# Linear attention in chunks of 64 tokens instead of 128, in smaller TensorE tiles, in a fused attention and mixture-of-experts layer

## What is computed

```python
h = layernorm(x)
q, k = elu(h @ Wq.T) + 1, elu(h @ Wk.T) + 1; v = h @ Wv.T      # 16 heads of 16 features
for each token t, each head:                                   # causal linear attention
    KV += outer(k[t], v[t]);  Ks += k[t]
    o[t] = (q[t] @ KV) / (q[t] . Ks + 1e-8)
x = x + o @ Wo.T
h = layernorm(x)
cw = top-4 of 8 experts, out of the best 2 of 4 groups, by sigmoid(h @ gate_w.T) + bias; scaled to sum 2.5
x = x + sum_e cw[e] * mlp_e(h) + mlp_shared(h)                 # mlp: silu(h@Wg) * (h@Wu) @ Wd, 128 wide
```

## Time and profile before

| | |
|---|---|
| median of 3 runs | 1036.24 us (1032.89 to 1036.34) |
| the profiled execution, by the same clock as the runs | 1035.56 us |
| its span, first to last instruction | 1033.8 us |
| PE busy | 1007.7 us (97%), 8437 matmul records |
| DVE busy | 873.0 us (84%) |
| POOL, ACT busy | 537.8 us (52%), 422.6 us (41%) |
| granted TensorE clock | full (2.4 GHz) in all slices |

### The profile page before, as it was taken

How to read it: one execution, slowest core, us unless ns; L and a number is a source line. 1 busy time by engine, 2 the same in 40 slices (tenths; PEclk the granted TensorE clock), 3 DMA queues, 4 the chain that set the end, 5 groups by cost and what they waited for, 6 DMA issues and landing times.

```text
span 1033.8 us, 22214 instructions
## 1 busy us (share of the span) xinstructions
PE 1007.7 (97%) x8437; PEld 858.1 (83%) x8437; DVE 873.0 (84%) x1855; ACT 422.6 (41%) x750; POOL 537.8 (52%) x440
## 2 busy tenths in 40 slices
PE   6889999999999999999999999999999999999997
PEld 5667878888888888888888888888888888888886
DVE  5988998898888889989898988889889898887564
ACT  5755343443434344343444434244343434422222
POOL 5763545636455564445646454564445546443653
PEclk9999999999999999999999999999999999999999
DMA  5011424444242443324435252443424345241511
GB/s 204 2 47 43 106 60 133 83 103 111 60 138 63 132 105 96 100 63 134 83 103 113 58 138 63 142 94 99 100 64 136 76 103 113 58 118 36 130 60 64
DMA packets 235161, 96.49 MB, mean 93 GB/s; under 512 B 161712, under 2 KB 217520, under 8 KB 235056
## 3 DMA queue, kind: packets, MB, share of 16 engines
q1 hardware_dynamic: 235056, 95.07, 36.0%
HBM read 66.60 MB, written 28.44 MB: 92 GB/s over the span
## 4 chain that ended last, share of the span: by engine, by line
PE 87%; DVE 6%; DMA 2%; ACT 1%; issue 1%; POOL 1%; SPq 1%; DVEq 0%; ACTq 0%
PE bank L989 53%; PE y_bank L989 19%; PE bank L1098 6%; PE bank L1114 5%; PE bank L1085 2%; PE bank L1128 2%; PE bank L1140 1%; DMA cw_all<-cw_dram 1%; DMA cw_all<-in_w_qkvo 1%; DVE scores L860 1%; DMA x_dram<-blocks 0%; DMA expo<-x_dram 0%; DVE den L869 0%; POOL et L729 0%; DVE et L957 0%
## 5 line engine op out<-in xcount | busy, mean ns | idle before, releaser
L989 PE MATMUL bank<-xt_hi,wg_hi 128*128 128x512 f32 x576 | 237.1, 412 | 3.0 <-DVE et L957 2.3
L989 PE MATMUL bank<-xt_hi,wg_lo 128*128 128x512 f32 x576 | 228.1, 396 | 0.0
L989 PE MATMUL bank<-xt_lo,wg_hi 128*128 128x512 f32 x576 | 227.8, 396 | 0.0
L732 POOL TENSOR_TENSOR h_lo<-et,h_hi 128x512 fp32r<-128x512 f32 x142 | 181.1, 1293 | 89.6 <-ACT h_hi L682 89.4
L729 POOL TENSOR_TENSOR et<-et,cw_all 128x512 f32<-128x512 f32 x126 | 166.2, 1338 | 112.6 <-DVE et L963 94.4
L860 DVE TENSOR_TENSOR scores<-bank,cst 128x512 f32<-128x512 f32 x240 | 152.6, 681 | 35.6 <-PE bank L1098 29.4
L989 PE MATMUL y_bank<-wd_hi,h_hi 128*128 128x256 f32 x576 | 164.9, 286 | 0.0
L989 PE MATMUL y_bank<-wd_lo,h_hi 128*128 128x256 f32 x576 | 162.1, 281 | 0.0
L989 PE MATMUL y_bank<-wd_hi,h_lo 128*128 128x256 f32 x576 | 161.3, 280 | 0.0
L989 PEld LDWEIGHTS bank<-xt_hi,wg_hi 128*128 128x128 f32 x576 | 108.3, 188 | 41.3 <-issue 16.6
L682 ACT ACTIVATE h_hi<-et 128x512 fp32r<-128x512 f32 x144 | 86.1, 624 | 116.7 <-POOL et L729 55.9
(11 more groups left out here) (135 smaller groups left out, 1870.5 us busy)
## 6 DMA issues: line engine op xcount, KB each, us to landing
cw_all<-cw_dram SPq DMA_DIRECT2D x128, 256.0 KB, 3.9
x_dram<-blocks SPq DMA_DIRECT2D x112, 128.0 KB, 3.3
out_y<-x_mid SPq DMA_DIRECT2D x32, 256.0 KB, 4.8
x_in<-in_x SPq DMA_DIRECT2D x15, 512.0 KB, 5.3
num_t<-x_dram SPq DMA_DIRECT2D x15, 512.0 KB, 4.0
expo<-x_dram SPq DMA_DIRECT2D x13, 512.0 KB, 4.0
k_dram<-blocks SPq DMA_DIRECT2D x52, 96.0 KB, 2.6
k_tok<-k_dram SPq DMA_DIRECT2D x13, 384.0 KB, 3.4
```

Source lines behind the costliest of these rows:

```text
L732: nc.gpsimd.tensor_tensor(h_lo[:, i % HR, :], et[:, i % ET, :], h_hi[:, i % HR, :].bitcast(f32), ALU.subtract).then_inc(h_lo_done, 1)
L989: ins = nc.tensor.matmul(dst, l, r, start=first and n == 0, stop=last and n == 2, skip_group_check=shared)
```

## The change

The chunk becomes 64 tokens (`CH`), eight of them. `scores` uses tiles of 32 rows x 64 columns: the pair g picks the row group, and even and odd chunks (r = 0, 1) pick the column half, that is partitions 0 to 63 or 64 to 127 of the bank of g. `values` uses 64 rows x 32 columns: r picks the row half and g the column group, and even and odd chunks write to banks of their own (`o` 2i + r). `state` is one entry now, in tiles of 64 x 32 with 32 streamed columns and two banks. `inter` uses tiles of 32 x 32 on the diagonal: pair g in row group g and column group g, seven chunks, even and odd chunks in the two `o` banks. The masks are 64 wide, so that there are 8 of 128 x 512 per batch in place of 16. DVE adds the seven states up in seven instructions. `k_turn` and `blocks.2`/`put.2`/`get.2` move four subtiles of k in place of three. `mult` is four instructions of 128 x 256 in place of two of 128 x 512. The last batch's weight rows 4 to 7 go to ring buffers of `scores`, once `values` of that batch is done with them, and wait for no `weigh`.

All order tables and `BANK` are written anew. One line of each, before and after:

```diff
-        up.6.3 down.3.3 state.1.1 down.4.3 scores.2.1 values.0.1 values.1.1 down.5.3 inter.0.1 inter.1.1
+        down.3.3 up.8.3 down.4.3 scores.1.1 down.5.3 down.6.3 values.0.1 values.1.1 router.0.2 inter.1.1
...
-        turn.0.0 turn.1.0 warm.17.0 v.1.0 k.0.0 q.0.0 v.0.0 k.1.0 q.1.0 scores.0.0 k_turn.0.0 scores.1.0
+        turn.1.0 turn.0.0 warm.21.0 k.0.0 q.0.0 q.1.0 k.1.0 warm.20.0 k_turn.1.0 k_turn.0.0 scores.0.0 v.0.0
...
-    ("o", 1): 2, ("q", 0): 5, ("q", 1): 5, ("router", 0): 1, ("scores", 0): 0, ("scores", 1): 4, ("scores", 2): 3,
+    ("o", 1): 5, ("o", 2): 1, ("o", 3): 3, ("q", 0): 2, ("q", 1): 4, ("router", 0): 0, ("scores", 0): 3,
```

The code (a line "..." stands where lines are left out):

```diff
+CH = P // 2
+CHUNKS = S // CH
...
     if name == "scores":
         return [("scores", 4 * i + g) for g in range(4)]
     if name == "values":
-        return [("o", i // 2)] if i % 2 == 0 else []
+        return [("o", 2 * i), ("o", 2 * i + 1)]
+    if name == "state":
+        return [("state", 0), ("state", 1)]
     return [(name, i)] if name in BANKED else []
+
+def product_range(*sizes):
+    return itertools.product(*(range(n) for n in sizes))
...
+        def cw_extra(k):
+            return scores[:, k, :, :].rearrange("p a q -> p (a q)")
...
+            k = slot_weights(i, b) - 1
+            if b == B - 1 and k >= CW:
+                wait_for(eng, cw_last[k - CW], 16)
+                return cw_extra(k)
+            n = E * b + k
...
+        def ring(i, b):
+            return scores[:, (PAIRS * b + i) % SM, :, :]
+        def wait_scores(eng, i, b):
+            before, j = divmod(PAIRS * b + i - SM, PAIRS)
+            if before >= 0:
+                wait_filled(eng, "values", j // 4, before)
...
-                        wait_weighed(sp, e % E + int(e // E < B - 1), e // E)
-                    sp.dma_start(cw_all[:, i % CW, :], cw_dram[b % 2, i].partition_broadcast(P))\
-                        .then_inc(cw_loaded[i % CW], 16)
+                    if b == B - 1 and i >= CW:
+                        wait_filled(sp, "values", 0, b)
+                        wait_filled(sp, "values", 1, b)
+                        dst, landed_sem = cw_extra(i), cw_last[i - CW]
+                    else:
+                        if E * b + i >= CW:
+                            before, j = divmod(E * b + i - CW, E)
+                            wait_weighed(sp, j + 1, before)
+                        dst, landed_sem = cw_all[:, i % CW, :], cw_loaded[i % CW]
+                    sp.dma_start(dst, cw_dram[b % 2, i].partition_broadcast(P)).then_inc(landed_sem, 16)
...
-                    dve.wait_ge(filled, FILLED["state", i, b])
-                    wait_filled(dve, "inter", 2 * i, b - 1)
-                    wait_filled(dve, "inter", 2 * i + 1, b - 1)
-                    nc.vector.tensor_tensor(st[:, i, :, :],
-                                            bank[BANK["state", i]][:, 0:(SUBS - 1) * P]
-                                            .rearrange("p (c n) -> p c n", n=P),
-                                            block_mask.unsqueeze(1).broadcast_to([P, SUBS - 1, P]), ALU.mult)\
-                        .then_inc(drained[BANK["state", i]], 1)
-                    dve.wait_ge(drained[BANK["state", i]], USES["state", i, b])
-                    nc.vector.tensor_tensor(st[:, i, 1, :], st[:, i, 0, :], st[:, i, 1, :], ALU.add)\
-                        .then_inc(state_done, 1)
-                    dve.wait_ge(state_done, 2 * STATE["state", i, b] - 1)
-                    nc.vector.tensor_tensor(st[:, i, 2, :], st[:, i, 1, :], st[:, i, 2, :], ALU.add)\
-                        .then_inc(state_done, 1)
+                    dve.wait_ge(filled, FILLED["state", 0, b])
+                    wait_filled(dve, "inter", 0, b - 1)
+                    wait_filled(dve, "inter", 1, b - 1)
+                    even, odd = (bank[BANK["state", r]][:, 0:CH * SUBS].rearrange("p (c n) -> p c n", n=CH)
+                                 for r in range(2))
+                    nc.vector.tensor_copy(st_sum[:, 0, :], even[:, 0, :])
+                    nc.vector.tensor_copy(st_sum[:, 1:6:2, :], odd[:, 0:3, :]).then_inc(drained[BANK["state", 1]], 1)
+                    dve.wait_ge(drained[BANK["state", 1]], USES["state", 1, b])
+                    link(nc.vector.tensor_tensor(st_sum[:, 1:6:2, :], st_sum[:, 1:6:2, :], even[:, 0:3, :], ALU.add))
+                    link(nc.vector.tensor_tensor(st_sum[:, 3, :], st_sum[:, 1, :], st_sum[:, 3, :], ALU.add))
+                    link(nc.vector.tensor_tensor(st_sum[:, 5, :], st_sum[:, 3, :], st_sum[:, 5, :], ALU.add))
+                    nc.vector.tensor_tensor(st_sum[:, 2:7:2, :], st_sum[:, 1:6:2, :], even[:, 1:4, :], ALU.add)\
+                        .then_inc(drained[BANK["state", 0]], 1)
+                    dve.wait_ge(drained[BANK["state", 0]], USES["state", 0, b])
+                    nc.vector.tensor_tensor(st[:, :, :, :].rearrange("p c m n -> p (c m) n"),
+                                            st_sum.rearrange("p c (m n) -> p (c m) n", m=KC),
+                                            head_mask.unsqueeze(1).broadcast_to([P, (CHUNKS - 1) * KC, 2 * DH]),
+                                            ALU.mult).then_inc(state_done, 1)
+                    dve.wait_ge(state_done, STATE["state", 0, b])
...
-                    for j in (2 * i, 2 * i + 1):
-                        dve.wait_ge(filled, FILLED["values", j, b])
-                        dve.wait_ge(filled, FILLED["inter", j, b])
+                    dve.wait_ge(filled, FILLED["values", i, b])
+                    dve.wait_ge(filled, FILLED["inter", i, b])
                     dve.wait_ge(rden_spread, SPREAD["spread", i, b])
-                    nc.vector.tensor_tensor(num_t[:, i, :], num_t[:, i, :], bank[BANK["o", i]][:, :], ALU.mult)\
-                        .then_inc(drained[BANK["o", i]], 1)
+                    num = num_t[:, i, :].rearrange("p (c r q) -> p c r q", r=2, q=CH)
+                    for r in range(2):
+                        nc.vector.tensor_tensor(num[:, :, r, :], num[:, :, r, :],
+                                                bank[BANK["o", 2 * i + r]][:, 0:S // 2]
+                                                .rearrange("p (c q) -> p c q", q=CH), ALU.mult)\
+                            .then_inc(drained[BANK["o", 2 * i + r]], 1)
...
                 elif name == "state":
...
-                    for c in range(SUBS - 1):
-                        last = nc.tensor.matmul(bk[:, c * P:(c + 1) * P].rearrange("p (g t d) -> p g t d", t=2, d=DH),
-                                                k_tok[:, i, c, :], v_win[:, c, i * 4:(i + 1) * 4, 0:3:2, :],
-                                                start=True, stop=True)
+                    for c, m, g, r in product_range(SUBS, KC, 4, 2):
+                        if 2 * c + r < CHUNKS - 1:
+                            half = slice(CH * r, CH * r + CH)
+                            last = nc.tensor.matmul(
+                                bank[BANK["state", r]][32 * g:32 * g + 32, CH * c + 32 * m:CH * c + 32 * m + 32]
+                                .rearrange("p (t d) -> p t d", t=2),
+                                k_tok[half, m, c, 32 * g:32 * g + 32], v_win[half, c, 4 * m + g, 0:3:2, :],
+                                start=True, stop=True)
                     last.then_inc(filled, 1)
                 elif name == "scores":
-                    m, c0 = i // 2, 2 * (i % 2)
-                    pe.wait_ge(drained[BANK["k", m]], USES["k", m, b])
-                    pe.wait_ge(q_half_done, Q_HALF["q_split", m, b])
-                    for j in range(2):
-                        cs = slice((c0 + j) * P, (c0 + j + 1) * P)
-                        for g in range(4):
-                            rows = slice(32 * g, 32 * g + 32)
-                            last = nc.tensor.matmul(
-                                bank[BANK["scores", 4 * i + g]][:, j * 2 * P:(j + 1) * 2 * P]
-                                .rearrange("p (h q) -> p h q", h=2),
-                                kf[rows, m, cs], q_half[rows, :, cs], start=True, stop=True)
-                            if j == 1:
-                                last.then_inc(filled, 1)
+                    pe.wait_ge(drained[BANK["k", i]], USES["k", i, b])
+                    pe.wait_ge(q_half_done, Q_HALF["q_split", i, b])
+                    for c, g, r in product_range(SUBS, 4, 2):
+                        rows, half = slice(32 * g, 32 * g + 32), slice(CH * r, CH * r + CH)
+                        cs = slice(P * c + CH * r, P * c + CH * r + CH)
+                        last = nc.tensor.matmul(
+                            bank[BANK["scores", 4 * i + g]][half, c * P:(c + 1) * P].rearrange("p (h q) -> p h q", h=2),
+                            kf[rows, i, cs], q_half[rows, :, cs], start=True, stop=True)
+                        if c == SUBS - 1 and r == 1:
+                            last.then_inc(filled, 1)
                 elif name == "values":
```

(28 more changed lines are left out.)

253 lines of the change are left out of this document (114 added, 139 removed).

## The result

| kernel | median us | runs |
|---|---|---|
| before | 1036.29 | 1032.89 to 1037.13, 4 runs |
| changed | 1076.28 | 1075.24 to 1076.86, 4 runs |

The changed kernel takes 1.039 times as long (95% interval 1.037 to 1.042): 40 us slower, where 982 us, 54 us faster, was forecast. Its profiled execution has a span of 1073.8 us. The page after: busy us of PE, its weight loads and DVE, the chain that ended last, PE's busy tenths and clock in 40 slices, and the instruction queues.

The account below looks back on a forecast made before the run. PE, busy 97% of the span, was taken to bound the kernel. From 1035.56 us, 42 for 13 STEPs, 7 for FIRST and 4.5 for LAST came off, giving 982 us; range for 8 in 10: 964 to 1028.

Parts of the forecast that it names:

- The durations of the blocks: PE blocks after the change: `scores` 0.9 us, `values` 1.8 to 2.4, `inter` 1.6, `state` 0.9 to 1.1.
- that rival: Slower rival on PE: each pass start costs 29 ns, a STEP 7.8 us longer, 1151 us in all; chance 0.06.
- `inter` serialized by its bank: Slower rival: four row groups writing one bank run one at a time, +4.7 us a STEP, about 1051 us; chance 0.08.
- a pass takes as long as it streams columns: PE pass time: 0.22 us at 256 columns, 0.11 at 128, extrapolated to 0.056 at 64, whatever its array rows and columns.
- The sum: PE time in a STEP at 9 ns a start: 6.6 + 1.8 = 8.4 us, 3.2 us less than before.
- The supply of instructions: Rival on PE's instruction fetches: one exposed for 2.6 us leaves 0.6 us gain a STEP, 1016 us; chance 0.11.
- Against: Argument against the supply rival: 64 `values` records and their 64 weight loads pass in 1.88 us without a gap.
- the 7 us forecast: Gain in FIRST from fewer masks and shorter attention: 7 us taken, bounds 3 to 10.
- DVE: DVE's work in a STEP: some 50 us of 58.6, 86% busy, no nearer to binding than before.
- The cover before `values`: Second-half `values` needs four masks (2.6 us) after `scores`, with 4 us of PE work between, called thin.
- LAST: Last stage: 2.5 us less from attention and 2 from the new weights row loads, 4.5 us in all.
- Two of the slower rivals: `inter` serialized by its bank, 1051 us, chance 0.08; and 29 ns a start, 1151 us, chance 0.06.

Follow-up runs that it names:

- the pair of series: Standalone kernel with series of 384 matmuls: `inter` tiles with one bank for four row groups, then a bank for each; 1.99 us either way.
- the series: Standalone kernels of 384-matmul series in several tile shapes, with idle DMA engines or beside a copy; least time from piece to piece 3.46 us.
- a run with more of its stands covered: Changed kernel with `values` halved and reordered in the STEPs, blocks of `values` and `inter` also apart in FIRST and LAST; 1032.75 us, ratio 0.998 to the kernel before.
- The rows alone: Kernel before with only the last batch's weights rows 4 to 7 loaded into free `scores` buffers, last batch 14 store behind them; 1032.6 us against 1035.42.

## Why the prediction was wrong

- **The durations of the blocks: right.** `scores` 1.2 us to its last end, `state` 1.16, 128 of `values` in 1.26 by starts, 56 of `inter` under 1.0. A start costs 10 ns, not 29: that rival is out, and so is `inter` serialized by its bank, as the pair of series shows. One reading of it was wrong without harm: "a pass takes as long as it streams columns", 0.056 us at 64, holds for the small tiles together (four of 14 ns are 0.056), but a pass of the whole array takes 0.11 us at 64 columns.
- **The step that failed:** "The sum leans on PE starting a pass each 7 ns for 1.8 us on end ... I take 9 ns". That PE can is right; that the instructions for it are there is not. The sum carried no term for it. It stood among the rivals, "The supply of instructions", but with "one fetch exposed for 2.6 us" in a STEP, 1016 us and a chance of 0.11. The size was off: the 384 passes of `values`, `router` and `inter` in a STEP are three pieces, and each takes 3.46 us or more where its passes take 1.3 to 1.8, so that it costs some 2 us, or more beside DMA traffic; the first is mostly covered by what stands ahead of it, two stands a STEP remain, and 55 us in all were measured. The argument "Against" it was the error in reading. 64 records of `values` "pass now in 1.88 us without a gap"; that is 27 to 29 ns a pass, just what the supply gives, and half a piece, and says nothing of 10 ns. I had the count (384 pairs, three fetches, in some 5 us) and did not ask how long one takes: at the 3.46 us or more of the series, three can't come in 5.
- **The clock** had no term either. It went to 1.2 GHz for a few us behind one stand of over 2 us or two shorter ones, in nine of 13 STEPs, which with one place in FIRST lost some 20 us. With most of the stands gone it is at 0.997, and at full speed in all the STEPs.
- **The sum redone:** 982 + 55 for stands + 20 for the clock = 1057; the profiled execution took 1076.0 (its span is 1073.8). By stage, FIRST, the STEPs and LAST were to take 94, 762 and 124.5 us and took 110.4, 840.6 and 122.8. In the STEPs, 79 us more: 46.5 are waits for "issue" and some 18 the clock. Most of the other 14 is how a stand is counted, from the modelled end of the last matmul, while without the stand the next one would have started before that end: 397.18 to 398.86 is 1.67 us from start to start where the profile has 1.46 idle, and over all of PE's gaps in the STEPs that adds up to some 12 us. In FIRST, 16 us more: 7 for "issue", under 2 for the clock, and the 7 us forecast did not come. What holds FIRST besides the stands was not settled; a run with more of its stands covered gained 1.3 us there.
- **DVE: right.** 670/13 = 51.6 us in a STEP for 50 forecast. The cover before `values` held, no wait names a mask there.
- **LAST: right.** The rows alone give 2.8 us, 2 forecast; the whole stage took 6 us less, 4.5 forecast.
- **Chances:** 0.85 lay at no change or faster. Two of the slower rivals were out by mechanism, and the true one stood on the faster side with its price too small.

## What to carry to other kernels

Count instructions as well as busy time: 128 passes of PE (256 instructions) need 3.5 to 4.0 us, up to 5.4 beside DMA traffic, or PE stands for the rest. So small tiles belong in blocks well under 128 passes with regular work between; 64 passes and 1.4 us of regular work left few stands here, and that order alone was worth 43 us. It only brought the kernel back to where it had been: an engine that is 97% busy can still be slower with less work in more instructions. And an order made without this cost has to be mended as a whole: three of my five reorderings made another engine late.
